# First close of a decoder layer: q, k and v in three float32r passes instead of float32, second bf16 parts on ScalarE

## The chip, the cores and the metric

The kernel runs on one core of one Trainium2 chip. The metric is device time of that core in microseconds (us), median of several runs; one more execution was taken with the hardware profiler. Engines are called TensorE (PE in the rows, PEld its weight loads), VectorE (DVE), ScalarE (ACT), GpSimd (POOL) and SyncE (SP, which only issues DMAs here).

## What is computed

One decoder layer for x of 4 x 1024 tokens with 256 channels: linear attention with random features, softmax attention with 154 memory positions, and a mixture of 16 experts, each added to its input and followed by a layer norm. The change lies between the first two:

```python
x = _layernorm(x + _L0_attn_ref(x, ...))        # first close: ends here ...
# _L0_xattn_ref:
qkv = x @ W_attn + b_attn                       # ... and computes this too
q, k, v = jnp.split(qkv, 3, axis=2)
```

`_L0_attn_ref` ends with `y @ W_proj + b_proj`, y being numerator over denominator for each head. The first close takes y and the reciprocal denominators from memory, multiplies, projects, adds x, normalises, stores the new x, and computes q, k and v of the next attention from it. q and k leave as three bf16 parts each, whose sum is the float32 value: the first is the value rounded, the second the rounded remainder, the third the rounded remainder of that. v leaves in float32 with a column of ones for each head.

## The kernel before

The program runs stages one after the other, with a barrier of all engines between them: a first projection (`pj` in the names of the rows), linear attention (`la`), the first close (`cl`, about 565 to 720 us), softmax attention (`sa`), the second close (`cl` too, at about 1545 us), and the experts (`mo`). `close_attention` writes both closes; `on` is true for the first.

A close works on 8 tiles of 512 tokens (4 batches, 2 halves), n = 0 to 7. Each engine has its own program in order; semaphores join them. For tile n:

- GpSimd multiplies y and the reciprocals (`yn`, L850) and adds x and bias (`xb`, L851), both 128x1024. It does this two tiles ahead: in the step of tile n it takes the root for tile n+1 (`rstd`, L857) and then `yn` and `xb` of tile n+2.
- TensorE, in each step: transposes of tile n (`ps_t`, L929), the output projection of tile n+1 (`ps_o`, L882), then q, k of tile n in four groups s = 0 to 3 of 128 columns (`ps_qk`, L893; s = 0, 1 are q and 2, 3 are k), then v (`ps_v`, L900). `ps_qk` has two buffers, so group s waits for the eviction of group s-2.
- ScalarE: issues the five loads of tile n+2 (`c_y` L194 twice, `c_inv` L197 twice, `c_x` L198; only for n up to 5), copies the transposed tile from PSUM (`xT`, L979), and evicts each group twice, as bf16 (`parts` 0, L990) and as float32 (`full`, L994), with the bias added.
- VectorE: sum and statistics of tile n+1 (`z` L1024, L701, L704, L706), split of s = 0, 1, normalisation of tile n+1 (`xn`, L1034), split of s = 2, 3, v with its bias (L1056). A split of a pair is: two remainders (`rest`, L1043), two casts to bf16 (second part, L1046), two subtractions for the third part (L1049).
- SyncE stores x of tile n, then the four groups of parts (384 KB each), then v in four pieces.

Semaphore `t_done` says that the transposed tile is in SBUF; `qk_full` and `qk_first` count evictions, `qk_split` the finished splits, `normed` the normalised tiles. `Chain` makes VectorE wait for its own earlier writes.

The first projection computes the same kind of product, q, k and v of the layer's first attention, in three passes (`three_passes`, L214 to L216): weights and x are split into a high part rounded to float32r and the rest, and high by low, low by high and high by high are added in PSUM. Its rows appear below as `pj_ps_qk`, `pj_w_lo`.

## Time and profile before

| | us |
|---|---|
| median of 3 runs (lowest, highest) | 2217.79 (2216.48, 2221.77) |
| the profiled execution, its own time | 2214.3 |
| its span, first to last instruction | 2212.2 |
| TensorE busy | 1867.3 (84%) |
| VectorE busy | 1486.7 (67%) |
| ScalarE busy | 912.7 (41%) |
| GpSimd busy | 389.1 (18%) |

The profiled execution lies 0.16% below the median. Mean granted TensorE clock is 0.925 of full. Busy time is the time in which an engine had an instruction at work; matmuls overlap, and one row of a matmul lasts longer than the distance to the next, so distances between starts are read for TensorE. In a row of the timeline the first number is the start, the second the length, x8 means eight such instructions merged, and the bracket gives the engine's idle time before and whom it waited for. A plain float32 matmul shows as two records, a float32r one as one.

### The profile page before, as it was taken

The page shows a single profiled execution, that of the slowest core. Times are in us where ns is not written, and L with a number is a line of the kernel's source. Part 1 is how long each engine was busy: PE and PEld are TensorE (multiplying, and loading weights), DVE is VectorE, ACT ScalarE, POOL GpSimd, SP SyncE. Part 2 cuts the span into 40 slices and gives each one's busy share as a digit, 9 for nine tenths or more (in the row PEclk, how much of TensorE's full clock was granted, in tenths as well). Part 3 has the DMA queues.
Part 4 walks back from the last instruction along what each step waited for, and adds up shares of the span by engine and source line. Part 5 has one row for each costly group of instructions (what it writes and reads, how often), then busy time and mean ns, then how long its engine had stood idle before and what let it go on. Part 6 is the DMA issues. An engine that isn't in the chain of part 4 may idle for free. (4 is left out here: it accounts for less than half of the span.)

```text
span 2212.2 us, 38875 instructions
## 1 busy us (share of the span) xinstructions
PE 1867.3 (84%) x13696; PEld 1218.1 (55%) x13696; DVE 1486.7 (67%) x3864; ACT 912.7 (41%) x1398; POOL 389.1 (18%) x511
## 2 busy tenths in 40 slices
PE   7914999999688058989989999956689999999997
PEld 4603766767455013333333333324478888888886
DVE  7921554555598167888878888523498877777776
ACT  5602554555233005656656666721333233323322
POOL 2110212110332501111111111255220000000000
PEclk9966999999899558999999999978899999999999
DMA  6961554543388410221222120336500000000000
GB/s 171 222 136 62 121 104 109 111 108 111 116 224 203 113 64 18 74 71 59 73 73 63 62 84 32 110 114 206 162 23 29 30 1 30 29 14 17 20 10 10
DMA packets 167359, 187.39 MB, mean 85 GB/s; under 512 B 80816, under 2 KB 137536, under 8 KB 161044
## 3 DMA queue, kind: packets, MB, share of 16 engines
q1 hardware_dynamic: 131456, 136.45, 21.4%
q0 software_dynamic: 18976, 28.01, 6.7%
q10 hardware_dynamic: 16756, 20.56, 3.5%
q8 instruction: 118, 1.93, 0.4%
q14 instruction: 53, 0.43, 0.1%
HBM read 114.33 MB, written 70.20 MB: 83 GB/s over the span
## 5 line engine op out<-in xcount | busy, mean ns | idle before, releaser
L1402 ACT ACTIVATE sa_prob<-sa_ps_s 128x1024 f32<-128x1024 f32 (+3 forms) x480 | 376.3, 825 | 337.2 <-PE sa_ps_s L1310 194.0
L1460 DVE CUSTOM_DVE_ANT_0 sa_ps_m<-sa_ps_m,sa_later 128x282 f32<-128x282 f32 (+4 forms) x640 | 278.5, 461 | 102.7 <-PE sa_ps_m L1283 101.4
L1463 DVE TENSOR_REDUCE sa_piece_max<-sa_ps_m 128x1 f32<-128x512 f32 x384 | 259.2, 688 | 36.6 <-PE sa_ps_m L1283 36.1
L1283 PE MATMUL sa_ps_m<-sa_k,sa_q 96*128 96x358 bf16 (+7 forms) x1024 | 259.4, 304 | 8.7 <-DVE sa_piece_max L1460 6.9
L1801 DVE SCALAR_TENSOR_TENSOR mo_acc<-mo_ps_o,mo_keep,mo_acc 128x256 f32<-128x256 f32 x512 | 212.2, 477 | 71.5 <-PE mo_ps_o L216 71.3
L1438 POOL TENSOR_SCALAR_AFFINE_SELECT sa_prob<-sa_prob 128x256 f32<-128x256 f32 x256 | 102.5, 406 | 579.6 <-ACT sa_prob L1402 576.7
L686 DVE TENSOR_TENSOR la_att<-la_ps_att,la_cap 128x512 f32<-128x512 f32 x128 | 88.3, 690 | 171.6 <-PE la_ps_att L587 171.6
L1667 ACT ACTIVATE mo_h_hi<-mo_h 128x512 fp32r<-128x512 f32 x144 | 91.0, 632 | 272.6 <-DVE mo_h L1783 270.4
L1281 PEld LDWEIGHTS sa_ps_m<-sa_km,sa_q 96*128 96x128 bf16 x512 | 50.7, 99 | 240.6 <-issue 146.6
L1281 PE MATMUL sa_ps_m<-sa_km,sa_q 96*128 96x154 bf16 x512 | 122.9, 245 | 70.3 <-DMA sa_q<-s_q_parts 51.2
L1310 PE MATMUL sa_ps_s<-sa_q,sa_k 99*128 99x512 bf16 (+3 forms) x768 | 180.4, 331 | 2.1 <-ACT sa_prob L1402 2.0
L639 ACT ACTIVATE la_phi_kT<-la_ps_kT 128x512 f32<-128x512 f32 x128 | 76.4, 597 | 246.3 <-PE la_ps_kT L568 163.8
L587 PE MATMUL la_ps_att<-la_phi_qT,la_phi_kT 128*128 128x128 f32 x1024 | 145.6, 286 | 33.0 <-ACT la_phi_qT L641 22.9
L1283 PEld LDWEIGHTS sa_ps_m<-sa_k,sa_q 96*128 96x128 bf16 x1024 | 98.9, 100 | 127.7 <-DVE sa_piece_max L1460 48.8
L214 PE MATMUL mo_ps_o<-mh_lo,mo_h_hi 128*128 128x256 f32 x576 | 162.8, 283 | 1.1 <-DVE mo_h_lo L1787 0.9
L215 PE MATMUL mo_ps_o<-mh_hi,mo_h_lo 128*128 128x256 f32 x576 | 163.1, 283 | 0.0
L216 PE MATMUL mo_ps_o<-mh_hi,mo_h_hi 128*128 128x256 f32 x576 | 163.1, 283 | 0.0
L1327 PE MATMUL sa_ps_y<-sa_prob,sa_v 128*17 128x512 f32 (+3 forms) x1536 | 160.2, 491 | 0.2 <-POOL sa_prob L1438 0.2
L1783 DVE TENSOR_TENSOR mo_h<-mo_silu,mo_ps_u 128x512 f32<-128x512 f32 x144 | 98.9, 687 | 83.5 <-PE mo_ps_u L216 80.7
L1663 ACT ACTIVATE mo_silu<-mo_ps_g 128x512 f32<-128x512 f32 x144 | 85.8, 596 | 159.4 <-PE mo_ps_g L216 159.2
L587 PEld LDWEIGHTS la_ps_att<-la_phi_qT,la_phi_kT 128*128 128x128 f32 x1024 | 126.9, 195 | 40.5 <-issue 37.1
L214 PE MATMUL mo_ps_g<-mo_x_lo,mh_hi 128*128 128x512 f32 x288 | 115.4, 401 | 26.7 <-DVE mo_h L1783 14.7
(197 smaller groups left out, 3835.7 us busy)
## 6 DMA issues: line engine op xcount, KB each, us to landing
s_y<-la_y SPq DMA_DIRECT2D x16, 512.0 KB, 2.9
s_x<-cl_xn SPq DMA_DIRECT2D x16, 512.0 KB, 6.1
s_y<-sa_y SPq DMA_DIRECT2D x16, 512.0 KB, 2.7
mw_raw<-experts SPq DMA_DIRECT2D x18, 384.0 KB, 4.5
s_q_parts<-pj_parts SPq DMA_DIRECT2D x16, 384.0 KB, 5.2
s_k_parts<-pj_parts SPq DMA_DIRECT2D x16, 384.0 KB, 2.6
s_q_parts<-cl_parts SPq DMA_DIRECT2D x16, 384.0 KB, 7.8
s_k_parts<-cl_parts SPq DMA_DIRECT2D x16, 384.0 KB, 6.8
```

The costliest lines, as they stand in the source:

```text
L214: nc.tensor.matmul(out, left[0], right[1], start=start, stop=False)
L215: nc.tensor.matmul(out, left[1], right[0], start=False, stop=False)
L216: return nc.tensor.matmul(out, left[0], right[0], start=False, stop=stop)
L587: last = nc.tensor.matmul(ps_att[:, j], phi_kT[:, d, j], phi_qT[:, d, j], start=True, stop=True)
L1281: nc.tensor.matmul(ps_m[:, s, 0:MEM], qs, km[g][0:STACK, j, 0:MEM], start=True, stop=True, skip_group_check=True)
L1283: last = nc.tensor.matmul(ps_m[:, s, a - lo:hi - lo], qs, k[g][0:STACK, j, a - MEM:hi - MEM], start=lo > 0, stop=True, skip_group_check=True)
L1310: last = nc.tensor.matmul(ps_s[:, s, jj, 0:TILE - first], keys, q[g][:, j, queries], start=True, stop=True)
L1327: last = nc.tensor.matmul(ps_y[32 * j:32 * j + V1, first:TILE], values, prob[:, prob_slot(g, units[j // 2]), j % 2, 0:TILE - first], start ...
L1402: nc.scalar.activation(dst, src, ACT.Exp, scale=HD ** -0.5).then_inc(expd[s], 1)
L1460: nc.vector.tensor_tensor_reduce(ps_m[:, s, 0:hi - lo], ps_m[:, s, 0:hi - lo], later[:, BANK + lo - first:BANK + hi - first], 1.0, -BIG, A ...
L1463: nc.vector.tensor_reduce(piece_max[:, j, t, n:n + 1], ps_m[:, s, 0:hi - lo], AX.X, ALU.max).then_inc(piece_done[s], 1)
L1801: last = nc.vector.scalar_tensor_tensor(acc[:, t], ps_o[:, s, t], keep[:, n * TB + t, i - 1:i], acc[:, t], ALU.mult, ALU.add)
```

## The change

- The weights of q, k and v are split once at the stage's start: `w_hi` (ScalarE, rounds to float32r), `w_lo` (VectorE, subtraction).
- The transposed tile is no longer copied as float32 (`xT` is gone in the first close). ScalarE writes `x_hi`, rounded to float32r, then VectorE writes `x_lo` = `ps_t` - `x_hi` in two subtractions (`rest_x`), and only then is `t_done` raised. `x_hi` and `x_lo` have one buffer each.
- q, k and v use `three_passes`: 6 matmul records for each group of q, k (4 before) and 6 for each of the four v pieces (4 before).
- The second bf16 parts are made by ScalarE (`second`), for a pair at a time, behind the eviction of the pair's later group. VectorE's subtraction for the third part waits for them.

```diff
@@ TensorE, qkv(b, half)
+                pe.wait_ge(w_split, 1 + START)
                 pe.wait_ge(t_done, n + 1 + START)
...
-                        last = nc.tensor.matmul(ps_qk[:, s % 2], w_qkv[:, a, s * P:(s + 1) * P], xT[:, half, a],
-                                                start=a == 0, stop=a == CT - 1)
+                        cols = slice(s * P, (s + 1) * P)
+                        last = three_passes(nc, ps_qk[:, s % 2], (w_hi[:, a, cols], w_lo[:, a, cols]), (x_hi[:, a], x_lo[:, a]),
+                                            start=a == 0, stop=a == CT - 1)
...
-                        last = nc.tensor.matmul(ps_v[:, t], xT[:, half, a, t * P:(t + 1) * P], w_qkv[:, a, 2 * C:3 * C],
-                                                start=a == 0, stop=a == CT - 1)
+                        tokens = slice(t * P, (t + 1) * P)
+                        last = three_passes(nc, ps_v[:, t], (x_hi[:, a, tokens], x_lo[:, a, tokens]),
+                                            (w_hi[:, a, 2 * C:3 * C], w_lo[:, a, 2 * C:3 * C]), start=a == 0, stop=a == CT - 1)
@@ ScalarE
+            if on:
+                nc.scalar.activation(w_hi[:, :, :], w_qkv[:, :, :], ACT.Copy).then_inc(w_hi_done, 1)
...
-                    if not on:
+                    if on:
+                        act.wait_ge(v_ps, n + START)
+                        nc.scalar.activation(x_hi[:, :, :], ps_t[:, :, :], ACT.Copy).then_inc(x_hi_done, 1)
+                    else:
                         act.wait_ge(stored_T[half], b * 16 + START)
-                    nc.scalar.activation(xT[:, half], ps_t[:, :, :], ACT.Copy).then_inc(t_done, 1)
+                        nc.scalar.activation(xT[:, half], ps_t[:, :, :], ACT.Copy).then_inc(t_done, 1)
...
                             nc.scalar.activation(full[:, s], ps_qk[:, s % 2], ACT.Identity,
                                                  bias=bias_qk[:, s:s + 1]).then_inc(qk_full[s % 2], 1)
+                            if s % 2:
+                                second(n, s - 1)
+                                second(n, s)
+
+            def second(n, s):
+                act.wait_ge(qk_rest, n * NS + s + 1 + START)
+                nc.scalar.activation(parts[:, s, 1], rest[:, s], ACT.Copy).then_inc(qk_second, 1)
@@ VectorE
+            if on:
+                dve.wait_ge(w_hi_done, 1 + START)
+                nc.vector.tensor_tensor(w_lo[:, :, :], w_qkv[:, :, :], w_hi[:, :, :].bitcast(F32), ALU.subtract).then_inc(w_split, 1)
+
+            def rest_x(b, half):
+                dve.wait_ge(x_hi_done, tile(b, half) + 1 + START)
+                for a in range(CT):
+                    last = nc.vector.tensor_tensor(x_lo[:, a], ps_t[:, a], x_hi[:, a].bitcast(F32), ALU.subtract)
+                last.then_inc(t_done, 1)
...
-                    ins = nc.vector.tensor_tensor(rest[:, s], full[:, s], parts[:, s, 0], ALU.subtract)
-                chain.link(ins)
+                    nc.vector.tensor_tensor(rest[:, s], full[:, s], parts[:, s, 0], ALU.subtract).then_inc(qk_rest, 1)
                 for s in pair:
-                    ins = nc.vector.tensor_copy(parts[:, s, 1], rest[:, s])
-                chain.link(ins)
-                for s in pair:
+                    dve.wait_ge(qk_second, tile(b, half) * NS + s + 1 + START)
                     nc.vector.tensor_tensor(parts[:, s, 2], rest[:, s], parts[:, s, 1],
                                             ALU.subtract).then_inc(qk_split[s % 2], 1)
...
+                    if on:
+                        rest_x(b, half)
                     if following:
                         sum_up(*following)
```

ScalarE between tile 0 and tile 1, before: evictions of the last group (L990 bf16, L994 float32), the five loads of tile 3, the copy of the transposed tile.

```order
L990 ACTIVATE cl_parts<-cl_ps_qk,c_bias_qk 128x512
L994 ACTIVATE cl_full<-cl_ps_qk,c_bias_qk 128x512
L194 DMA c_y<-s_y 128x1x512 x2
L197 DMA c_inv<-s_inv 128x1x512 x2
L198 DMA c_x<-x 128x4x256
L979 ACTIVATE cl_xT<-cl_ps_t 128x1024
```

The same place now (L1003 and L1007 are the evictions, L1015 the second parts, L989 the high part of x).

```order
L1003 ACTIVATE cl_parts<-cl_ps_qk,c_bias_qk 128x512
L1007 ACTIVATE cl_full<-cl_ps_qk,c_bias_qk 128x512
L1015 ACTIVATE cl_parts<-cl_rest 128x512 x2
L194 DMA c_y<-s_y 128x1x512 x2
L197 DMA c_inv<-s_inv 128x1x512 x2
L198 DMA c_x<-x 128x4x256
L989 ACTIVATE cl_x_hi<-cl_ps_t 128x1024
```

The two second parts of k stand ahead of the loads, and they wait for VectorE's remainders.

VectorE in the step of tile 1, before, from the sum of the next tile to its normalisation.

```order
L1024 TENSOR_TENSOR cl_z<-cl_ps_o,cl_xb 128x512 x2
L701 BN_STATS cl_stats<-cl_z 128x6 x4
L704 BN_AGGR cl_moments<-cl_stats 128x2 x4
L706 TENSOR_SCALAR cl_var<-cl_moments 128x4
L1041 REGISTER_ALU
L1042 ISA
L1043 TENSOR_TENSOR cl_rest<-cl_full,cl_parts 128x512
L1042 REGISTER_ALU
L1043 TENSOR_TENSOR cl_rest<-cl_full,cl_parts 128x512
L1046 CAST cl_parts<-cl_rest 128x512 x2
L1049 TENSOR_TENSOR cl_parts<-cl_rest,cl_parts 128x512 x2
L1032 ISA
```

Now:

```order
L1065 TENSOR_TENSOR cl_x_lo<-cl_ps_t,cl_x_hi 128x512 x2
L1039 ISA
L1044 TENSOR_TENSOR cl_z<-cl_ps_o,cl_xb 128x512 x2
L701 BN_STATS cl_stats<-cl_z 128x6 x4
L704 BN_AGGR cl_moments<-cl_stats 128x2 x4
L706 TENSOR_SCALAR cl_var<-cl_moments 128x4
L1071 REGISTER_ALU
L1072 ISA
L1073 TENSOR_TENSOR cl_rest<-cl_full,cl_parts 128x512
L1072 REGISTER_ALU
L1073 TENSOR_TENSOR cl_rest<-cl_full,cl_parts 128x512
L1076 TENSOR_TENSOR cl_parts<-cl_rest,cl_parts 128x512 x2
```

The low part of x has come ahead of the sum, and the two casts between the remainders and the third parts are gone.

## Rows read from the trace of the kernel before

**Rows 1.** Windows, the stretch around the first close; columns as in the first line.
```profile
core 0: us, PE busy (x) PEld busy (x) DVE busy (x) ACT busy (x) POOL busy (x), PEclk, DMA share, GB/s
...
560.00:730.00 170.00, 127.33 (x448) 84.09 (x448) 126.05 (x253) 48.65 (x72) 50.89 (x25) 0.91 0.70 183
```

**Rows 2.** Windows, cut at each tile's first q, k matmul; two steps left out.
```profile
585.00:603.00 18.00, 15.10 (x59) 10.06 (x58) 16.58 (x31) 6.08 (x9) 6.60 (x3) 1.00 0.42 124
603.00:622.50 19.50, 16.52 (x57) 11.01 (x56) 16.94 (x32) 6.08 (x9) 6.70 (x3) 0.91 0.90 231
...
658.10:675.70 17.60, 15.41 (x57) 9.70 (x56) 15.51 (x32) 6.08 (x9) 6.10 (x3) 1.00 0.92 253
675.70:695.30 19.60, 16.81 (x57) 11.12 (x56) 16.43 (x32) 6.08 (x9) 6.51 (x3) 0.91 0.69 200
695.30:707.80 12.50, 11.39 (x42) 6.85 (x40) 11.28 (x28) 6.08 (x9) 1.30 (x1) 1.00 0.74 149
```

**Rows 3.** Timeline of one step, all engines: start, length, engine, line, operation.
```profile
597.15 1.38 DVE L1034 TENSOR_SCALAR cl_xn<-cl_z,cl_moments,cl_rstd 128x256 f32<-128x256 f32 x4
598.44 1.29 DVE L1043 TENSOR_TENSOR cl_rest<-cl_full,cl_parts 128x512 f32<-128x512 f32 x2
...
598.58 1.10 PE L929 MATMUL cl_ps_t<-c_ident,cl_xn 128*128 128x128 f32 x8 [2.90 <-DVE cl_xn L1034]
...
599.72 1.02 ACT L979 ACTIVATE cl_xT<-cl_ps_t 128x1024 f32<-128x1024 f32 x1 [6.19 <-PE cl_ps_t L929]
599.77 0.76 DVE L1046 CAST cl_parts<-cl_rest 128x512 bf16<-128x512 f32 x2
...
602.97 7.03 PE L893 MATMUL cl_ps_qk<-cl_xT,c_w_qkv 128*128 128x512 f32 x16
...
606.70 1.43 POOL L857 TENSOR_TENSOR cl_rstd<-cl_var,cl_power 128x4 f32<-128x4 f32 x1 [11.08 <-DVE cl_var L706]
...
608.11 2.79 POOL L850 TENSOR_TENSOR cl_yn<-c_y,c_inv 128x1024 f32<-128x1024 f32 x1
...
608.72 4.96 DVE L1046 CAST cl_parts<-cl_rest 128x512 bf16<-128x512 f32 x2
...
610.86 2.54 POOL L851 TENSOR_TENSOR cl_xb<-c_x,c_bias 128x1024 f32<-128x1024 f32 x1
...
614.93 1.38 DVE L1034 TENSOR_SCALAR cl_xn<-cl_z,cl_moments,cl_rstd 128x256 f32<-128x256 f32 x4
```

**Rows 4.** Timeline, a remainder beside GpSimd's product.
```profile
662.92 2.35 POOL L850 TENSOR_TENSOR cl_yn<-c_y,c_inv 128x1024 f32<-128x1024 f32 x1
...
664.15 1.66 DVE L1043 TENSOR_TENSOR cl_rest<-cl_full,cl_parts 128x512 f32<-128x512 f32 x1 [1.43 <-ACT cl_full L994]
```

**Rows 5.** Timeline of the first projection, two passes of three in a row.
```profile
43.28 0.40 PE L215 MATMUL pj_ps_qk<-pj_x_hi,pj_w_lo 128*128 128x512 f32 x1
...
43.52 0.39 PE L216 MATMUL pj_ps_qk<-pj_x_hi,pj_w_hi 128*128 128x512 f32 x1
```

**Rows 6.** Groups by line, 560 to 730 us: count, busy us, mean ns, idle before.
```profile
L990 ACT ACTIVATE cl_parts<-cl_ps_qk,c_bias_qk 128x512 bf16<-128x512 f32 x32 | 22.0, 687 | 48.2 <-PE cl_ps_qk L893 39.8 <-DMA s_q_parts<-cl_parts 6.7 <-DMA s_k_parts<-cl_parts 1.8
L994 ACT ACTIVATE cl_full<-cl_ps_qk,c_bias_qk 128x512 f32<-128x512 f32 x32 | 21.7, 679 | 0.0
```

**Rows 7.** Timeline, ScalarE's queue: first and last of five loads.
```profile
610.38 0.65 ACTq L194 DMA_DIRECT2D c_y<-s_y  x1
...
613.85 0.39 ACTq L198 DMA_DIRECT2D c_x<-x  x1
```

**Rows 8.** DMA queue of the loads in 622 to 624 us: packets, MB, share.
```profile
q10 hardware_dynamic: 60, 0.05, 8.9%
```

**Rows 9.** Instructions that write pj_w_lo: count, min, median, max ns.
```profile
L416 DVE TENSOR_TENSOR pj_w_lo<-pj_w,pj_w_hi x1: 1758/1758/1758, 10.6 to 10.6; 128x1536 fp32r<-128x1536 f32 x1
```

**Rows 10.** Timeline at the stage's start, GpSimd and VectorE.
```profile
571.47 2.35 POOL L851 TENSOR_TENSOR cl_xb<-c_x,c_bias 128x1024 f32<-128x1024 f32 x1
572.21 1.29 DVE L1024 TENSOR_TENSOR cl_z<-cl_ps_o,cl_xb 128x512 f32<-128x512 f32 x2 [4.24 <-PE cl_ps_o L882]
```

**Rows 11.** Window of one us in the step of 603 to 622.5 us.
```profile
618.00:619.00 1.00, 1.00 (x4) 0.82 (x3) 0.97 (x3) 0.59 (x1) 0.00 (x0) 0.50 1.05 303
```

More of the change, by code:

```diff
@@ L730, in close_attention @@
         xn = ph.sb("xn", [P, HALVES, TB, C])
-        xT = ph.sb("xT", [P, HALVES, CT, TILE])
+        xT = None if on else ph.sb("xT", [P, HALVES, CT, TILE])
         stats, moments = ph.sb("stats", [P, TB, 6]), ph.sb("moments", [P, TB, 2])
@@ L744, in close_attention @@
             w_qkv, bias_qk, bias_v = closing.w_qkv, closing.bias_qk, closing.bias_v
+            w_hi, w_lo = ph.sb("w_hi", [P, CT, 3 * C], F32R), ph.sb("w_lo", [P, CT, 3 * C], F32R)
+            x_hi, x_lo = ph.sb("x_hi", [P, CT, TILE], F32R), ph.sb("x_lo", [P, CT, TILE], F32R)
+            w_hi_done, w_split, x_hi_done = ph.sem("w_hi_done"), ph.sem("w_split"), ph.sem("x_hi_done")
             full = ph.sb("full", [P, NS, TILE])
@@ L751, in close_attention @@
             qk_ps, v_ps, qk_first = ph.sem("qk_ps"), ph.sem("v_ps"), ph.sem("qk_first")
+            qk_rest, qk_second = ph.sem("qk_rest"), ph.sem("qk_second")
             qk_full = ph.sems("qk_full", 2)
```

## The prediction

> **What bounds the kernel now.** I read the busy time by stage first. The first close runs from 565 to 720 us, and in the stretch around it no engine is full [rows 1]: TensorE 127 us of 170, VectorE 126, ScalarE 49, DMA share 0.70. So an engine's sum decides nothing here; a chain between engines does. Cut tile by tile, from the first q, k matmul of a tile to that of the next, the first five steps take 90.7 us, 18.1 each. VectorE is busy for 15.5 to 16.9 us of each, the DMA share is up to 0.92, and the two steps of 19.5 and 19.6 us are those with a granted clock of 0.91 [rows 2].
>
> The timeline of one step shows the chain [rows 3]. Call N the start of the normalisation of the next tile and q its first q, k matmul. N is 597.15, the transposes follow at 598.58, then the output projection of the tile after, which fills TensorE until q at 602.97, so N to q is 5.8 us. ScalarE's copy of the transposed tile is done at 600.74, 2.2 us before it is wanted. From q, VectorE does the sum and the statistics, GpSimd the root (606.70), and the next N is 614.93: q to N is 11.96 us. In this second half lies the dearest thing of the stage: VectorE's two casts to bf16 start at 608.72 and take 4.96 us together, while the same two take 0.76 us at 599.77. Beside the slow pair GpSimd runs its two 128x1024 products and sums (608.11 and 610.86), and the pair ends 0.3 us after the second. Two rows tell whether this belongs to casts alone: a subtraction that reads two SBUF tensors, 0.65 us when undisturbed, starts at 664.15 and takes 1.66 us; it ends 0.5 us after the GpSimd operation that ran from 662.92 to 665.27 [rows 4]. It waited too, and got its turn between two GpSimd operations.
>
> **Removed from TensorE.** A q, k group is 4 records of 0.43 us now (16 in 7.03, [rows 3]), 1.72 us. The three-pass form stands in the first projection of this kernel: one pass of 128x512 starts every 0.23 us [rows 5], so six take 1.40 us, 0.32 less. It moves the first result of a tile 0.3 us forward. But after q the chain waits for sum, statistics and root (q + 3.6), and the first result is evicted (two activations of 0.69 and 0.68, the second 0.6 behind the first, [rows 6]) by q + 2.9. The v part is shorter as well and ends before N. Worth on the chain: nothing, except in the last tile, where four groups give 4 x 0.32 = 1.3 us.
>
> **Casts leave VectorE.** One would count 5.7 us a tile. What is left in their place is the third part's subtraction, which reads two SBUF tensors and waits like the one in [rows 4]. From q: results out by q + 2.9 and q + 4.35; statistics done at q + 3.4; remainders q + 3.45 and q + 4.4 (0.69 each); ScalarE's second part of the first is ready near q + 5.0. GpSimd's root ends at q + 5.0 (606.70 + 1.43 is 602.97 + 5.16) and its product takes the port. The two subtractions then get a turn each, after the product and after the sum: 5.0 + 2.34 + 0.69 + 2.34 + 0.65 = q + 11.0 for N against q + 11.96. The cut is worth 0.9 us, not 5.7.
>
> The skill states this as a rule: the Trainium skill, SBUF — State Buffer, section "Who interferes with whom", says that a VectorE instruction with two SBUF inputs contends with a GpSimd instruction that reads SBUF, and that the loser waits for all of the other. The trace agrees (1.66 us for 0.65).
>
> **Second parts on ScalarE.** Two activations of 0.6 us stand after each pair. The first pair delays the third result by 1.2 us, in time that ends before N. The second pair is what costs. ScalarE is in order, and the five loads of the tile after next are issued behind it: they now start when the fourth remainder is ready, and that is computed after N (two take 1.29 from N + 1.29), so at N + 2.65. Today they go out ahead of N (610.38 to 614.24 against 614.93) in 3.9 us [rows 7]; over five tiles the mean is 3.6, which I take. Behind them stands the copy of the transposed tile. So from N: 2.65 + 3.6 issue + 1.02 copy.
>
> **New: the low part of x on VectorE.** Two operations that read PSUM and SBUF, like the sum (1.29 for two), 1.29 us, between the copy and the matmuls. All before q: 2.65 + 3.6 + 1.02 + 1.29 + 0.2 of handovers = N + 8.8, against N + 5.8. The slack of 2.2 us is eaten, 3.0 are left over. A step with loads: 11.0 + 8.8 = 19.8.
>
> **When do the loads land?** The product needs them. Loads issued at 610.38 to 614.24 still move 8.9% in 622 to 624 and nothing in the two after them [rows 8], so about 9.3 us after the last issue, and that was mostly ahead of the output traffic. From N + 6.3 that is N + 15.6, q + 6.8, later than the root. Then both subtractions pass first, N comes at q + 6.5, but GpSimd's pair (q + 6.8 to q + 12.2 with a turn between) catches the remainders behind N, the fourth ends at q + 12.8, and issue, copy and low part follow: 6.2 more, a step of 19.0. The two orders give nearly the same. I take 19.3, which is 1.2 above 18.1.
>
> **The sum.** Steps with loads: 5 x 1.2 = +6.0. The sixth has no loads: N to q is then 1.29 + 1.29 + 0.65 + 0.65 + 1.41 + 1.29 and handovers = 6.7, with 11.0 that is 17.7 against 19.6 [rows 2]: -1.9. The seventh has no GpSimd pair: 13.0 against 12.5, +0.5. Last tile -1.3. At the start the low part of the weights takes 1.76 us [rows 9] and stands ahead of the first sum (572.21). It reads two SBUF tensors, so it gets its turn when GpSimd passes from one operation to the next at 571.5 (ScalarE's copy of the weights, by its 1.02 us for 1024 columns some 1.5 us, is ready by then), and ends at 573.3 [rows 10]: +1.0. Together +4.3.
>
> **Clock.** TensorE now idles 2.9 us in a step, ahead of the transposes [rows 3]. In two of six steps its granted clock was at the lower level (0.50, which is 1.2 GHz) for a while after that [rows 2, 11], and these two steps are 1.7 us longer than their neighbours. After the change it idles about 3.8 us before the transposes and 2.5 before q. Bounds: no step more than now (0) and all seven, 5 more x 1.7 = 8.5, or at worst 2 us for each, 14. I take 4, since the slow output projection is hidden by the longer N to q but slow q groups aren't. Sum: +8.3 us. Against the profiled execution (span 2212.2, its time 2214.3) that is 2222.6; the median of the runs is 2217.8, and 8.3 on it is **2226**.
>
> **Rivals.**
> (a) Late landing helps. The loads now share the queues with q, k parts from the start. If they land later than q + 9.7, the remainders pass ahead of GpSimd too and a step is held by the DMA engines alone: 0.92 x 17.6 = 16.2 us [rows 2], say 16.5. For: the outputs now start with the loads and not after them, and in today's steps the engines already stand at 0.9 [rows 2]. Against: it needs 3 us beyond the 9.3 measured. 5 x -1.6, -3 in the sixth, +1.0 + 0.5 - 1.3: about -11, 2207.
> (b) Only casts wait. The subtraction of [rows 4] would be an exception, N comes at q + 6.4 and the step at 15.2 is again held by DMA, 16.2: with the sixth at 14, -15 us, 2203. In a sentence of its own: the Trainium skill, Perfetto Trace Analysis, section "Optimizing Scalar/DVE Operations", says that when VectorE is saturated, moving work to ScalarE may make sense; by that rule this is the case that comes true. Against: 1.66 us for a 0.65 us operation.
> (c) Slower than the forecast: the clock falls in every step. TensorE is busy 13 us of 19.3 where it was 15 of 18.1. If q starts at the lower level each time, the first group takes 2.8 us instead of 1.4, the remainder misses its place before GpSimd, and a step is 2 us longer: +4.3 + 14 = +18, 2236. It decides where the lower level (0.50) still stands when q begins; today it was over by then [rows 2].
> (d) The chain is as told, but issue and lock overlap better: a step of 18.4, near no change: +0 to +5, 2220.
>
> **Chances.** Forecast 0.45 (own range 2221 to 2232), (d) 0.15, (c) 0.15, (a) 0.15, (b) 0.10. A measurement tells about 0.3%, 6.7 us, from no change. Faster by more: (a) mostly and (b), 0.23. Same: (d), the lower part of the forecast, a bit of (a), 0.29. Slower: 0.48. The range takes in (a) and (c) and leaves out (b) and what lies beyond: 2206 to 2238.
>
> **What would show it.** Right: ScalarE's load issues behind the second-part activations and after N; ScalarE's idle time before its x copy put down to nothing or to its own queue, not to TensorE; subtractions for the third part with 2 to 3 us instead of 0.65 beside GpSimd; the x copy no longer 2 us ahead of the output projection's end; steps of 19 to 20 us. Wrong: subtractions of 0.65 us beside GpSimd operations (b), GpSimd's product waiting for its loads beyond q + 9 with steps of 16.5 us (a), or q groups that start at the lower clock in each step (c).

## The result, and the profile after

The changed kernel takes 2226.67 us (median of 19 runs), the kernel before 2218.1 us beside it (19 runs). The ratio is 1.0035, with a 95% interval of 1.0024 to 1.0046, so the change costs about 8 us. The forecast was 2226.

The profiled execution of the changed kernel is at the high end of its runs (its time is 2233.33 us, its span 2231.6), so the distance between the two profiles, 19.4 us, is more than the medians show. Where it lies is read from four instructions that mark stages: the first clear of the close (`cl_v`), the first of the softmax stage (`sa_piece_max`), and the first and last copy of scores in the second close (`cl_scoreT`). Instructions by tile; behind the name stand count, shortest, median and longest ns, then the first and last start. The kernel before, then after:

```profile
L1008 DVE MEMSET cl_v<- x1: 165/165/165, 562.6 to 562.6; 128x128 f32 x1
L1444 DVE MEMSET sa_piece_max<- x1: 138/138/138, 728.6 to 728.6; 128x96 f32 x1
L984 ACT ACTIVATE cl_scoreT<-cl_ps_r x8: 586/586/587, 1491.9 to 1559.6; 32x512 f32<-32x512 f32 x8
```

```profile
L1028 DVE MEMSET cl_v<- x1: 165/165/165, 565.2 to 565.2; 128x128 f32 x1
L1473 DVE MEMSET sa_piece_max<- x1: 138/138/138, 738.5 to 738.5; 128x96 f32 x1
L997 ACT ACTIVATE cl_scoreT<-cl_ps_r x8: 586/586/589, 1504.7 to 1579.3; 32x512 f32<-32x512 f32 x8
```

The first close takes 173.3 us, 7.3 more than before (166.0). It starts 2.6 us later, the softmax stage between the closes takes 766.2 against 763.3, and the second close 74.6 against 67.7. Start and second close don't belong to the change: the start lies ahead of the edited stage and falls anywhere between 558 and 565 us in the profiles of this study, and a second profile of the unchanged kernel (the last experiment below) shows 166 us again for the first close, but 76.4 for the second. For the softmax stage that isn't certain. It takes 760.6 to 763.7 us in the five profiles with the plain matmuls, e2 below left out, and 762.7 to 767.2 in the seven with the three passes, so some of its 2.9 us may come with the change; no run looked into that.

The windows of the changed kernel, as in [rows 1, 2]: the whole first close, then steps from one tile's first q, k matmul to the next one's (the first, second, fifth, sixth and seventh; the cuts lie up to 0.3 us ahead of the matmuls).

```profile
565.20:738.50 173.30, 120.60 (x576) 99.55 (x576) 126.37 (x237) 67.61 (x105) 53.16 (x25) 0.87 0.66 178
588.87:608.70 19.83, 15.23 (x74) 12.60 (x73) 16.60 (x30) 8.36 (x13) 6.95 (x3) 0.91 0.35 98
608.70:625.80 17.10, 13.48 (x72) 11.07 (x72) 16.22 (x30) 8.25 (x13) 7.25 (x3) 1.00 0.91 250
...
663.80:684.10 20.30, 13.44 (x72) 11.15 (x72) 16.49 (x30) 8.25 (x13) 6.28 (x3) 0.97 0.75 213
684.10:704.60 20.50, 17.06 (x71) 14.07 (x72) 16.35 (x29) 8.13 (x13) 6.17 (x3) 0.78 0.63 188
704.60:717.80 13.20, 10.04 (x59) 8.39 (x58) 12.14 (x29) 8.33 (x13) 1.30 (x1) 0.98 0.82 192
```

VectorE has some 15 instructions fewer in the close and is as busy as before (126 us): what the casts gave up came back as waiting inside its other instructions. The timeline of the first step shows it. It answers to [rows 3, 7], and the columns are the same.

```profile
594.11 3.50 DVE L1076 TENSOR_TENSOR cl_parts<-cl_rest,cl_parts 128x512 bf16<-128x512 f32 x2
...
594.26 2.81 POOL L854 TENSOR_TENSOR cl_yn<-c_y,c_inv 128x1024 f32<-128x1024 f32 x1
...
597.03 2.79 POOL L855 TENSOR_TENSOR cl_xb<-c_x,c_bias 128x1024 f32<-128x1024 f32 x1
...
597.54 3.40 DVE L1054 TENSOR_SCALAR cl_xn<-cl_z,cl_moments,cl_rstd 128x256 f32<-128x256 f32 x4
...
600.86 1.28 DVE L1073 TENSOR_TENSOR cl_rest<-cl_full,cl_parts 128x512 f32<-128x512 f32 x2
...
601.57 1.23 ACT L1015 ACTIVATE cl_parts<-cl_rest 128x512 bf16<-128x512 f32 x2 [4.53 <-DVE cl_rest L1073]
602.18 1.26 ACTq L194 DMA_DIRECT2D c_y<-s_y  x2
...
605.38 0.80 ACTq L198 DMA_DIRECT2D c_x<-x  x1
606.28 1.02 ACT L989 ACTIVATE cl_x_hi<-cl_ps_t 128x1024 fp32r<-128x1024 f32 x1 [3.47 <-issue]
607.33 1.29 DVE L1065 TENSOR_TENSOR cl_x_lo<-cl_ps_t,cl_x_hi 128x512 fp32r<-128x512 f32 x2 [2.48 <-ACT cl_x_hi L989]
...
608.72 0.47 PE L214 MATMUL cl_ps_qk<-cl_x_lo,cl_w_hi 128*128 128x512 f32 x1 [1.49 <-issue]
```

One of the two third parts waits for GpSimd's product. Then the normalisation waits too, for the sum. The two second parts follow the remainders behind it, and only then ScalarE issues the loads, 4.6 us behind the start of the normalisation (597.54; N, as in the prediction, with q for a tile's first q, k matmul), where before they went out ahead of it. Behind the issues stand the copy of x, its low part and the matmuls. Over the whole close, groups by line (the window is 560 to 740 us; busy us, mean ns, then idle time before them) and waits (us in all, times, longest):

```profile
L1076 DVE TENSOR_TENSOR cl_parts<-cl_rest,cl_parts 128x512 bf16<-128x512 f32 x32 | 32.1, 1020 | 1.4
L1054 DVE TENSOR_SCALAR cl_xn<-cl_z,cl_moments,cl_rstd 128x256 f32<-128x256 f32 x32 | 21.2, 726 | 1.3 <-POOL cl_rstd L861 1.3
```

```profile
ACT cl_x_hi L989 <- issue: 18.1, 5, 3.9
...
POOL cl_yn L854 <- DMA c_x<-x: 15.6, 5, 4.1
...
PE cl_ps_qk L214 <- DVE cl_x_lo L1065: 13.3, 4, 5.8
...
DVE cl_x_lo L1065 <- ACT cl_x_hi L989: 11.6, 5, 3.1
```

ScalarE's copy of x waits five times behind the issue of loads and no longer for TensorE alone, GpSimd waits five times for loads that land late, the low part of x waits for its copy, and TensorE four times for the low part.

### The profile page after: what moved, and what is told of

It is laid out like the page before. It is cut to its first block and busy times, and to the rows that moved or that the text cites. A ratio compares the mean times of both kernels' runs of the same rounds, so it can differ in the third digit from the quotient of the medians.

```text
span 2231.6 us, 39166 instructions
## 1 busy us (share of the span) xinstructions
PE 1871.3 (84%) x13824; PEld 1240.7 (56%) x13824; DVE 1483.3 (66%) x3849; ACT 931.6 (42%) x1431; POOL 391.4 (18%) x511
## 5 line engine op out<-in xcount | busy, mean ns | idle before, releaser
L639 ACT ACTIVATE la_phi_kT<-la_ps_kT 128x512 f32<-128x512 f32 x128 | 76.4, 597 | 248.9 <-PE la_ps_kT L568 165.7
```

## The experiments

Each run is told by its median, its ratio to the kernel before on the same chip, and the length of the first close in its profile (166.0 before, 173.3 after). The medians are of 19 executions for the changed kernel and of 4 (e9) to 12 for the others, the close of one profile each.

| kernel | median us | ratio to before (95% interval) | first close us |
|---|---|---|---|
| after | 2226.67 | 1.0035 (1.0024 to 1.0046) | 173.3 |
| e1 split alone | 2229.61 | 1.0046 (1.0033 to 1.0058) | 175.4 |
| e2 second parts on ScalarE alone | 2233.22 | 1.0051 (1.0037 to 1.0065) | 160.4 |
| e9 the same, straight code | 2208.0 | 0.9954 (0.9937 to 0.9970) | 158.3 |
| e10 before, straight code | 2218.86 | 0.9996 (0.9985 to 1.0007) | 165.6 |
| e11 after, straight code | 2224.93 | 1.0028 (1.0016 to 1.0039) | 170.4 |
| e3 after, loads ahead | 2219.33 | 0.9992 (0.9975 to 1.0010) | 166.4 |
| e7 after, no low part of x | 2212.66 | 0.9968 (0.9952 to 0.9985) | 162.2 |
| e4 after, product and sum late | 2222.77 | 1.0011 (1.0002 to 1.0021) | 171.3 |
| e5 before, sum late | 2209.2 | 0.9956 (0.9941 to 0.9970) | 156.4 |
| e6 e3 with the sum late | 2206.26 | 0.9945 (0.9925 to 0.9964) | 156.4 |
| e8 before again | 2221.13 | 1.0010 (0.9995 to 1.0025) | 165.8 |

### One half alone: the split of x and weights

The changed kernel with the second parts back on VectorE.

```diff
-                            if s % 2:
-                                second(n, s - 1)
-                                second(n, s)
...
+                for s in pair:
+                    ins = nc.vector.tensor_copy(parts[:, s, 1], rest[:, s])
+                chain.link(ins)
                 for s in pair:
-                    dve.wait_ge(qk_second, tile(b, half) * NS + s + 1 + START)
```

> The changed kernel with the second bf16 parts back on VectorE: only the three passes, the split of weights and x. Theory (the low part of x joins VectorE's own chain of remainders, casts, third parts and v): from N to q it is 1.34 + 1.29 + 0.76 + 1.29 + 1.41 + 1.29 = 7.4 us where it was 5.8, q to N stays 12.0, so about 1.4 us for each of 7 steps, 1.0 at the start, -1.3 in the last tile: 8 to 10 us above the kernel before, 2226 to 2228. The loads go out before N again, and ScalarE waits for the transposes ahead of its x copy. Rival 1 (only the loads behind the second parts cost something): within 2 us of the kernel before.

Measured: 2229.61 us. The three passes alone cost 10 us (0.46% of 2219). The timeline of one step of this kernel shows where, in two places:

```profile
598.92 1.37 DVE L1046 TENSOR_SCALAR cl_xn<-cl_z,cl_moments,cl_rstd 128x256 f32<-128x256 f32 x4
600.21 1.28 DVE L1065 TENSOR_TENSOR cl_rest<-cl_full,cl_parts 128x512 f32<-128x512 f32 x2
...
602.11 5.60 PE L885 MATMUL cl_ps_o<-c_w,cl_yn 128*128 128x256 f32 x16
...
602.36 1.02 ACT L988 ACTIVATE cl_x_hi<-cl_ps_t 128x1024 fp32r<-128x1024 f32 x1 [7.54 <-PE cl_ps_t L935]
603.53 1.41 DVE L1078 TENSOR_TENSOR cl_v<-cl_ps_v,c_bias_v 128x256 f32<-128x256 f32 x4
604.86 1.28 DVE L1057 TENSOR_TENSOR cl_x_lo<-cl_ps_t,cl_x_hi 128x512 fp32r<-128x512 f32 x2
...
607.36 0.58 PE L214 MATMUL cl_ps_qk<-cl_x_lo,cl_w_hi 128*128 128x512 f32 x1
```

ScalarE's copy is done at 603.38, and the low part starts 1.5 us later: it stands in VectorE's queue behind all k parts and the evictions of v. N to q is at least 1.38 + 1.29 + 0.76 + 1.29 + 1.41 + 1.29 = 7.4 us by VectorE alone, against 5.8 before. The copy itself waits for TensorE only, and no load stands ahead of it.

The second place is TensorE's clock. In this step N to q is 8.4 us and not 7.4: the low part ends at 606.14, and TensorE goes over to q at 607.36 without a wait, straight from the output projection. That takes 5.3 us from its first matmul to q, against 3.5 in the same step before (599.52 to 602.97); the granted clock from 602.0 to 607.3 is 0.61, and TensorE had idled for 4.0 us ahead of the transposes (2.9 before). The mean granted clock is 0.83 in two of the six steps and 0.91 in the other four, where before it is 1.00 in four and 0.91 in two. In those four steps the low part ends 0.1 to 0.3 us ahead of q, and in the other two 1.2 and 1.3 us. The 9.4 us of the close are 0.5 up to the first q of the second tile, 5.6 in six steps, 2.0 in the seventh and 1.3 in the last tile, whose first 4.4 us run at a granted clock of 0.50. No run tells what the low part would cost at an unchanged clock.

### The other half alone, and why its first run misled

The kernel before with the second parts on ScalarE.

```diff
+                            if s % 2:
+                                second(n, s - 1)
+                                second(n, s)
...
-                for s in pair:
-                    ins = nc.vector.tensor_copy(parts[:, s, 1], rest[:, s])
-                chain.link(ins)
                 for s in pair:
+                    dve.wait_ge(qk_second, tile(b, half) * NS + s + 1 + START)
```

> The kernel before with the second bf16 parts on ScalarE, float32 matmuls kept. Theory: q to N falls to 11.0 (third parts wait for GpSimd in place of the casts), N to q rises from 5.8 to 7.4 (2.65 until the fourth remainder, 3.6 load issue, 1.02 copy), the sixth and seventh step gain 1 and 0.5: between -1 and +3 us to the kernel before. Rival (only casts contend with GpSimd): VectorE is free 5.7 us earlier, steps are held by the DMA engines at 16.2: -10 us or more. Rival 2 (the second parts on ScalarE are the whole loss): +8.

Measured: 2233.22 us, slower than the kernel before, and by its median than the changed kernel too (there the intervals overlap), though the first close became 5.6 us shorter. The whole loss and more is in the softmax stage, whose code is untouched: 779.9 us, 16.6 above before. Its waits on ScalarE, and the longest of them in the timeline:

```profile
ACT sa_prob L1407 <- issue: 18.2, 4, 5.7
```

```profile
1320.71 1.94 ACT L1407 ACTIVATE sa_prob<-sa_ps_s 128x1024 f32<-128x1024 f32 x2 [5.68 <-issue]
```

ScalarE stood still four times with nothing to wait for. The list of DMA queues on the profile's page gave a hint, a queue for instructions that moved more here than in any other kernel of this study (packets, MB, share):

```profile
q14 instruction: 69, 0.57, 0.1%
```

In the kernel before it has 53 packets. To tell work from place, the same edit was run with ScalarE's loop turns of the first close written out, and the same was done to the kernels before and after as controls.

```diff
             row(0, True, True)
-            with act.Fori(1, B - 1) as b:
-                row(b, False, True)
+            if on:
+                for b in range(1, B - 1):
+                    row(b, False, True)
+            else:
+                with act.Fori(1, B - 1) as b:
+                    row(b, False, True)
```

> The kernel before with the second parts on ScalarE, as in the run e2_act_only, and with one thing more: ScalarE's two loop turns of the first close are written out as straight code, so that its instructions behind them stand at other places in its program. The work is the same. In e2_act_only the first close took 160.4 us (165.9 before) but the softmax stage 779.9 us (763.3 before), with ScalarE there idle for its own instructions (18.2 us in 4 places) and 69 packets on the instruction queue against 53 to 55. Theory 1, the idle time is a matter of where the loops stand in ScalarE's program: the softmax stage is back at 762 to 767 us, no such wait and 53 to 56 packets, the first close stays at 158 to 163 us, and the median is 2218 - 5.5 = 2212 (2209 to 2216). Theory 2, the second parts on ScalarE cost the stage behind in any place: the softmax stage stays near 780 us and the median near 2230. A result of 2217 to 2224 with a softmax stage of 763 would say that the 5.5 us of the first close were chance.

> The kernel before with only ScalarE's two loop turns of the first close written out as straight code. It is the control for e9_act_unrolled (2208.0 us, 0.9954 of before) and e3_loads_ahead (0.9992), which both have that change too. Theory 1, straight code is worth nothing and the 10 us of e9 are those of the second parts on ScalarE: 2217 to 2221 us, first close 165 to 167 us. Theory 2, the loop turn costs ScalarE what e9 gained: 2208 to 2211, first close near 160 us. Rival, the code behind is shifted into a bad place as in e2_act_only: 2230 and more, with ScalarE idle for its own instructions in the softmax stage.

> The kernel after with only ScalarE's two loop turns of the first close written out as straight code; the loads stay behind the second parts. It is the control for e3_loads_ahead (2219.3), which has the loads ahead and the straight code. Theory 1, the 7 us of e3 are those of the place of the loads: this run gives 2225 to 2229 us, first close 171 to 175 us. Theory 2, they are those of the straight code: 2218 to 2221, first close 166 to 168 us.

Measured: 2208.0 us, 2218.86 us and 2224.93 us. In the first the softmax stage takes 762.7 us again, no wait of `sa_prob` for issue is left, and the queue is back at

```profile
q14 instruction: 54, 0.44, 0.1%
```

So the 16.6 us were a matter of how the code is laid out, not of the work, and the straight code by itself is worth nothing (e10) or at most 2 us (e11, inside the intervals). What the second half of the change is worth alone is a **gain of 10 us**, 0.46%. Its close is 7.3 us shorter than that of its control, so about 3 of the 10 us are not seen in the edited stage. I read the reason as the landing; no run moves it alone. The loads go out behind the second parts, and GpSimd waits for them; rows of e9, waits and groups:

```profile
POOL cl_yn L851 <- DMA c_x<-x: 23.5, 5, 7.4
ACT cl_xT L980 <- issue: 14.2, 5, 3.6
```

```profile
L1046 DVE TENSOR_SCALAR cl_xn<-cl_z,cl_moments,cl_rstd 128x256 f32<-128x256 f32 x32 | 11.0, 407 | 1.3 <-POOL cl_rstd L858 1.3
```

From the second step on the product comes so late that the q parts and the normalisation pass ahead of it (407 ns, undisturbed), and the pair meets the k parts behind N instead. From the third step on N starts 7.0 us behind the sum of z or less, where it is 11.7 in the control e10, and the longer way from N to the next sum (9.4 to 10.6 us) eats only a part of that. The order isn't safe: in e2, with the same work, the normalisation of the fifth step met GpSimd's pair and took 5.56 us, that step 20.9 us and the close 2.1 us more than in e9.

The two halves cost +10 and -10 alone, and +8 together: 8 us of the gain are lost in the combination. By the length of the close it is +9.4 and -7.3 alone, and +7.3 together (+4.8 in the pair with straight code, e11 and e10), so 3 to 5 us of the loss are seen in the stage itself.

### The loads ahead of the second parts

The changed kernel, with the next tile's loads issued behind the last eviction and ahead of the second parts of k.

```diff
+                            if s == NS - 1 and n + 1 < (B - 1) * HALVES:
+                                load_inputs(act, *divmod(n + 1, HALVES))
                             if s % 2:
                                 second(n, s - 1)
```

> The changed kernel with ScalarE issuing the next tile's five loads behind the last eviction and ahead of the two second parts of k (ScalarE's loop over batches written out). Theory: the issue is hidden in the wait for the remainders, the copy of x comes 3 us earlier, a step is 11.0 + 6.7 = 17.7 instead of 19: 6 to 8 us below the changed kernel, 2218 to 2221. Rival (the loads' landing or the DMA engines hold the steps): within 2 us of the changed kernel.

Measured: 2219.33 us, 7 below after and level with before. The copy of x no longer waits for issues:

```profile
L987 ACT ACTIVATE cl_x_hi<-cl_ps_t 128x1024 fp32r<-128x1024 f32 x8 | 8.2, 1021 | 11.0 <-PE cl_ps_t L936 10.9
...
L1059 DVE TENSOR_SCALAR cl_xn<-cl_z,cl_moments,cl_rstd 128x256 f32<-128x256 f32 x32 | 23.2, 784 | 1.3 <-POOL cl_rstd L861 1.3
```

Control e11 gives up to 2 of the 7 us to the straight code; about 5 belong to the order (the close is 4.0 us shorter than that of e11). Now the product is never late, and the normalisation meets GpSimd in six of seven steps (784 ns against 407): one loss went, and the other grew. The clock comes in as in e1: in all six steps TensorE idles 3.0 to 3.2 us ahead of the transposes, the mean granted clock is 0.82 to 0.91, and q follows the output projection without a wait, 0.5 to 2.1 us behind the end of the low part.

### The low part of x taken away

The changed kernel, but the low part of x is written once, from weights, and never again; so this kernel leaves the low part of x out of its result. The matmuls still do all three passes.

```diff
-                        nc.scalar.activation(x_hi[:, :, :], ps_t[:, :, :], ACT.Copy).then_inc(x_hi_done, 1)
+                        nc.scalar.activation(x_hi[:, :, :], ps_t[:, :, :], ACT.Copy).then_inc(t_done, 1)
...
-                    if on:
-                        rest_x(b, half)
```

> The changed kernel without the low part of x: x_lo is written once at the start with other data, and the matmuls may start behind ScalarE's rounded copy; everything else, the loads behind the second parts too, is as in the changed kernel. Theory (1.3 us of x_lo stands on the chain of each step): 5 to 8 us below the changed kernel, 2219 to 2222. Rival (x_lo is hidden beside the output projection or the steps are held by GpSimd and the loads): less than 2 us below.

Measured: 2212.66 us, 14 below after and lower than the 2219 to 2222 that were expected; the close is 11.1 us shorter. The part is 1.29 us per tile, 10.3 us for all eight. Like steps show that it lay on the chain: where the product comes behind the normalisation three steps take 14.9 to 15.5 us, against 17.3 and 17.7 in the changed kernel, and where the two meet 18.8 and 19.0 against 19.9 to 20.5. (A fourth step of the first kind takes 19.2: its output projection waits 2.9 us for the product and then runs at a granted clock of 0.51.) The order of events shifted as well: the normalisation meets GpSimd in two steps and not in four, so its group is

```profile
L1054 DVE TENSOR_SCALAR cl_xn<-cl_z,cl_moments,cl_rstd 128x256 f32<-128x256 f32 x32 | 15.1, 533 | 1.3 <-POOL cl_rstd L861 1.3
```

against 21.2 us in the changed kernel. The mean of the normalisation is 726 ns in after, 533 in e7 and 407 in e9. As I read these three, this is where a part of e9's gain is lost: the low part lengthens the way from the copy to N, while the landing doesn't move with it, and the product stands in front of the normalisation more often. But e11, which does the same work as after, has 598 ns, so how often they meet changes by itself by a good part of that difference. The way from cause to order was not tested by itself.

### GpSimd behind the k parts

The changed kernel, with product and sum held until VectorE's k parts are done.

```diff
                 wait_summed(pool, tile(b, half), 2)
+                if on and late is not None:
+                    pool.wait_ge(qk_split[1], use(*late, NS - 1) + 1 + START)
                 nc.gpsimd.tensor_tensor(yn[:, half], y[:, half], inv[:, half], ALU.mult).then_inc(scaled, 1)
```

> The changed kernel in which GpSimd begins its product and sum for the tile after next only when VectorE has finished the k parts of the current tile, so that the two run beside v, the low part of x and the statistics. Theory (VectorE operations with two SBUF inputs wait for GpSimd): no third part longer than 0.8 us, q to N falls from 11 to 6.5, a step is 15.3 and then held by the DMA engines at 16.2 to 16.8: 12 to 18 us below the changed kernel, 2209 to 2215. Rival (the long third parts have another cause, or loads' landing is what counts): less than 4 us below the changed kernel.

Measured: 2222.77 us, where 2209 to 2215 were expected. The contention is gone, and something else has come; groups by line, then the timeline of one step:

```profile
L888 PE MATMUL cl_ps_o<-c_w,cl_yn 128*128 128x256 f32 x128 | 47.7, 553 | 27.8 <-POOL cl_yn L856 27.8
...
L1078 DVE TENSOR_TENSOR cl_parts<-cl_rest,cl_parts 128x512 bf16<-128x512 f32 x32 | 21.5, 690 | 1.2
```

```profile
611.79 1.38 DVE L1056 TENSOR_SCALAR cl_xn<-cl_z,cl_moments,cl_rstd 128x256 f32<-128x256 f32 x4
...
618.32 5.40 PE L888 MATMUL cl_ps_o<-c_w,cl_yn 128*128 128x256 f32 x16 [3.17 <-POOL cl_yn L856]
...
623.84 1.29 DVE L1046 TENSOR_TENSOR cl_z<-cl_ps_o,cl_xb 128x512 f32<-128x512 f32 x2 [2.16 <-PE cl_ps_o L888]
```

The third parts take 690 ns where they took 1020, and the normalisation 1.38 us for four again: in all some 20 us of VectorE's time. But the product is wanted at once. The output projection could start behind the transposes, here at 615.15, and starts at 618.32; it now waits 27.8 us for the product in all (9 of them at the stage's start, as in every kernel), and N to the next sum of z is 12 to 13 us. The projection also runs at a granted clock of 0.52 to 0.68. I had taken the product to be a step early. Only GpSimd's sum has time to spare, since VectorE reads it behind the output projection. So the second form holds the sum alone.

```diff
                 nc.gpsimd.tensor_tensor(yn[:, half], y[:, half], inv[:, half], ALU.mult).then_inc(scaled, 1)
+                if on and late is not None:
+                    pool.wait_ge(qk_split[1], use(*late, NS - 1) + 1 + START)
                 nc.gpsimd.tensor_tensor(xb[:, half], x[:, half], bias[:, :, :], ALU.add).then_inc(biased, 1)
```

> The kernel before with one wait more on GpSimd: its sum of x and bias for the tile after next begins when VectorE has finished the k parts of the current tile; root and product stay where they are. Theory (what holds a step is GpSimd's pair in front of VectorE's casts): one turn of waiting instead of two, q to N falls from 12.0 to about 10, N to q stays near 6, a step is 16.1, which is also about what the DMA engines allow: 9 to 12 us below the kernel before, 2207 to 2210. Rival (the DMA engines or the landing of loads already hold the steps at 17.8): within 3 us of it.

> The changed kernel with both: loads issued ahead of the second parts of k, and GpSimd's sum behind VectorE's k parts. Theory: no turn of GpSimd falls on the normalisation, q to N is about 8, N to q 6.7, a step 15 to 16.5: 8 to 13 us below the kernel before, 2206 to 2211, and the same as the kernel before with the late sum within 3 us. Rival (three passes cost VectorE too much): 5 us or more above that one.

Measured: on the kernel before 2209.2 us, on e3 2206.26 us. Both times are as expected and both beat the kernels before and after. In the kernel before with this edit one turn at the port is left of two:

```profile
605.59 2.35 POOL L850 TENSOR_TENSOR cl_yn<-c_y,c_inv 128x1024 f32<-128x1024 f32 x1
605.70 2.78 DVE L1045 TENSOR_TENSOR cl_rest<-cl_full,cl_parts 128x512 f32<-128x512 f32 x1 [0.97 <-ACT cl_full L996]
608.52 0.76 DVE L1048 CAST cl_parts<-cl_rest 128x512 bf16<-128x512 f32 x2
```

The two casts take 0.76 us here, where they took 4.96 in [rows 3]; a remainder waits once, 2.78 us for 0.69. (In three of the six steps it is the casts that wait once, 2.79 to 2.92 us.) The way to the time was not quite the one expected: q to N is 10.3 to 11.3 us in five of six steps, not about 10, since the sum of z now starts 1.4 us behind q, where it started 0.2 to 0.3 us behind it: it waits for GpSimd's sum. And a part of the gain is the clock. TensorE idles less than 1 us ahead of the transposes, N to q is 5.8 to 5.9 us in all six steps at a granted clock of 1.00, and the two steps of the kernel before with 7.6 and 7.5 us, at a lower clock, don't occur; that is 3.4 of the 9.6 us by which the close became shorter. Without the sum in the way the whole change, with its loads ahead, costs nothing against the plain form: the closes of e5 and e6 are both 156.4 us long, and the distance of their medians, 3 us, is inside the intervals.

### The kernel before, once more

No edit.

> The kernel before, unchanged, for a second trace: which stages differ between two executions of the same program. Theory: the first close lasts 164 to 168 us again, and the second close, which took about 68 us in the first trace and 73 to 75 us in all other kernels so far, varies with the landing of its loads and may take 74 here too. Rival (the second close is slower because of the change): it takes 68 again.

Measured: 2221.13 us. Its second close, to be set beside that of the first profile:

```profile
L984 ACT ACTIVATE cl_scoreT<-cl_ps_r x8: 587/587/589, 1489.2 to 1565.6; 32x512 f32<-32x512 f32 x8
```

The first close takes 165.8 us again and ends at the same 728.6. The second takes 76.4 us, not 67.7, in the same kernel. Such a stage can't be held against an edit from one profile of each.

## Why the prediction was right, point by point

**The chain and its price.** Right. The parts of the first close, from the marks above and each tile's first q, k matmul, beside those of the forecast (whose 4 us for the clock are a term of their own):

| part | forecast | measured | how |
|---|---|---|---|
| start to the second tile's q | +1.0 | +1.1 | 588.87 - 565.2 = 23.7 against 585.20 - 562.6 = 22.6 |
| five steps with loads | +6.0 | +4.9 | 684.31 - 588.87 = 95.4 against 675.71 - 585.20 = 90.5 |
| sixth step | -1.9 | +0.9 | 20.5 against 19.6 |
| seventh | +0.5 | +0.6 | 13.0 against 12.5 |
| last tile and end | -1.3 | -0.1 | 20.7 against 20.8 |
| clock | +4 | in the parts above | |
| sum | +8.3 | +7.3 | 8.5 by the medians |

That the sum comes within 1 us is partly luck. The steps with loads cost 1.1 us less than forecast, sixth step and last tile 2.8 and 1.2 us more, the 4 us for the clock had no place of their own, and inside the steps a loss that was put at nothing (the normalisation, below) stands against one that was put too high (the wait of the third parts).

**Loads behind the second parts.** Right, with the row that was named: the copy of x waits 18.1 us for issues, and e3 gets about 5 us back by the order alone. **Late landing.** It was named as the second order of a step, with N at q + 6.5, and four of the five steps have it (in the second, q is at 608.72 and N at 615.15). The product starts 10.7 us behind the last issue (606.18), where 9.3 was worked out. That it would be worth as much as the first order was right for the sum only. A step in which only N comes early takes 17.3 us (the second), one in which N then meets GpSimd 20.3 (the fifth). Rival (a) needed a landing beyond q + 9.7; the product started at q + 8.1 (616.86). In e9 it starts at q + 8.2 to q + 10.2, the steps from the third to the sixth take 16.2 to 16.9 us, and the time is 2208, near that rival's 2207. I take that to say that it was nearer than 0.15.

**Low part of x.** The price of 1.29 us on the chain was right as far as it went, but it was told as 3.0 us of lengthening behind a slack of 2.2 on ScalarE's side. By e1 the slack doesn't help: the part stands behind VectorE's own queue, and the three passes cost 10 us even where the loads are early, though the lower clock has a share in that which no run separates.

**Casts.** That the cut is worth 0.9 us and not 5.7 in a step where GpSimd runs beside it holds for the first step: the third parts take 3.50 us and the normalisation behind them 3.40, and it ends 12.1 us behind q (588.87), where 11.0 and 1.38 were worked out. Both third parts were done in one turn, though, and N stood at q + 8.7, not at q + 11.0: it was the normalisation that paid the second turn. Rival (b), only casts wait, is out by the 1020 ns of the third parts. But the prediction gave this half of the change only its costs. Alone it gains 10 us (e9), as I read it through the later landing that it causes. That gain was not seen; it was weighed only as a rival of the whole change.

**Normalisation.** Missed. It was left at 1.38 us, and it takes 3.40 to 5.48 beside GpSimd in four steps, 10.2 us in all (21.2 against 11.0). The size was hidden in the sum since the second turn at the port had been charged to the third parts instead. The Trainium skill, SBUF — State Buffer, section "Who interferes with whom", lists tensor_scalar among the operations that can enter a two-port mode and then contend; the 3.40 us agree, though [rows 3] had shown it undisturbed only.

**Sixth step.** The term that was most off, by 2.8 us. Without loads it was to be 17.7. Two things came in: its matmuls started at the lower clock, as did those of the last tile, and its normalisation met GpSimd (3.40 for 1.38). Windows at the start of the sixth step and of the last tile, columns as above, and two rows from the sixth step:

```profile
684.30:686.90 2.60, 2.59 (x6) 2.12 (x7) 2.53 (x9) 0.00 (x0) 0.00 (x0) 0.50 0.90 213
...
717.80:719.80 2.00, 1.99 (x5) 1.61 (x6) 0.00 (x0) 0.00 (x0) 0.00 (x0) 0.50 1.06 224
```

```profile
691.82 3.70 DVE L1076 TENSOR_TENSOR cl_parts<-cl_rest,cl_parts 128x512 bf16<-128x512 f32 x2
...
692.57 2.40 POOL L854 TENSOR_TENSOR cl_yn<-c_y,c_inv 128x1024 f32<-128x1024 f32 x1 [4.06 <-DMA c_x<-x]
```

Ahead of the sixth start TensorE had idled for its longest wait, 5.8 us for the low part of x; a granted clock of 0.50 is 1.2 GHz. The first remainder of that tile starts at 688.76, 4.5 us behind the first matmul (684.31), where q + 3.45 was worked out and q + 3.2 measured in the four steps before; the second starts 6.9 us behind it, against 4.4 in the fifth step. So one third part is still open when the product lands (692.57, q + 8.3) and waits for it, and N comes at q + 11.1, 4.7 us later than in each of the four steps before. That is rival (c)'s own way, the remainder that misses its place before GpSimd, in one step, and a start at the lower clock in two of eight. The last tile's gain of 1.3 us came to 0.1. How much of the sixth step is the clock's, no run tells. The -1.9 also rested on the 19.6 us that the sixth step took in one profile: in e8 and e10, the same work, it takes 17.8, and the lower clock falls on the fifth.

**Three passes.** Right: worth nothing on the chain. TensorE is busy 120.6 us of the close for 127.3 before and its saving shows nowhere. What the prediction's "the slow output projection is hidden by the longer N to q" says holds for the changed kernel, where q waits for the low part in four steps; in e1 and e3, where it doesn't, q follows the slow projection. The mean granted clock of the close is 0.92 before, 0.87 after, 0.84 in e1 and 0.85 in e3.

## What to carry to other kernels

Where an in-order queue holds both small work and the issue of loads, a new wait ahead of the loads shifts their landing too, and whether that helps or hurts hangs on who stands at the shared port when they land; look for the one operation that is wanted last (here GpSimd's sum) and put it behind the rest, which gave 10 us with the plain matmuls and 10 (by the close and by the ratios) to 13 (by the medians) with the three passes. Read TensorE's granted clock step by step as well: a chain that leaves it idle longer ahead of its transposes had a slower projection behind them here (e1, e3), and one that shortened the idle time had none (e5). Run each half of a change alone, since +10 and -10 looked like +8. When a run is off by more than the edited stage can give, read the stages that weren't edited before forming a theory.

## What was not expected of the hardware

- ScalarE can stand still for its own instructions, four times and 18.2 us in all, in a stage far behind the edit. It came with 69 packets on the instruction queue instead of 53 to 55, and went when the same work was laid out as straight code. What rule decides where it happens stays open.
- The normalisation, one SBUF tensor in and one out with two scalars per row, waits for GpSimd like the subtractions of two tensors: 3.40 and 5.48 us for 1.38.
- What stands beside GpSimd's pair gets a turn between its two operations (third parts 3.50, then the normalisation 3.40 in the first step), so that two queued operations can delay two of VectorE's in a row; in these traces that happened to casts, third parts, remainders and the normalisation.
- TensorE's granted clock and the idle time ahead of the transposes go together in these traces. Six steps with 0.7 to 1.0 us of it ran at 1.00 up to q (e5), of six with 1.8 to 3.0 us two fell to the lower level, 0.50 or 1.2 GHz, for a while (before, 0.91 over the step), and with 3.0 to 3.2 us (e3) or 3.9 to 4.1 us (e1) all six did.
- The second close takes 67.7 us in one profile of the kernel before and 76.4 in another. Why was not looked into.
